# A two-layer graph network on one Trainium2 core: loop heads at the first slot of a fetch block, and basis values and window in PSUM

## The reference, cut to what matters

```python
basis = _basis(pseudo)                                   # edges x 9
messages = jnp.einsum('ek,ei,kio->eo', basis, x[row], weight)
out = jnp.zeros(...).at[col].add(messages)
out = out / jnp.maximum(degree, 1.0)[:, None]
out = out + x @ root_w.T + root_b

R = relu(abs_distances[:, None] @ w1 + b1) @ w2 + b2     # layer 2, per edge
acc = acc + _NORM[i] * jnp.einsum('euv,ef,evi,ofi->euo', Rb[..., k], Yf, Fb, C)
out = out.at[dst].add(msg)

x = _layernorm(x + layer1(x)); x = _layernorm(x + layer2(x))
```

## Time and profile before

| | us |
|---|---|
| median of 3 runs | 11979.86 (11974.05 to 11981.97) |
| the profiled execution | 12073.65 |
| span of its trace | 12071.8 |
| loop 1 (L363 first to L379 last) | 122.07 to 4941.83 |
| loop 2 | 5229 to 11990, about |

### The profile page before, as it was taken

How to read it: one execution, slowest core, us unless ns; L and a number is a source line. 1 busy time by engine, 2 the same in 40 slices (tenths; PEclk the granted TensorE clock), 3 DMA queues, 4 the chain that set the end, 5 groups by cost and what they waited for, 6 DMA issues and landing times. The chain is left out here.

```text
span 12071.8 us, 141219 instructions
## 1 busy us (share of the span) xinstructions
PE 8509.0 (70%) x44451; PEld 5928.2 (49%) x44451; DVE 5978.8 (50%) x14666; ACT 947.4 (8%) x3157; POOL 6732.9 (56%) x6757
## 2 busy tenths in 40 slices
PE   5777777777777777646666666666666667666676
PEld 5777777777676777523333333333333333333333
DVE  4333332333232323375666656566666666666665
ACT  0000000000000000001011011011101111110110
POOL 5777777677776777234444444444444444444442
PEclk5555555555555555578888888888888888888887
DMA  1000000000000000111111111111111111111111
GB/s 35 11 11 11 11 11 11 10 11 11 10 11 10 11 11 10 36 31 38 38 37 39 37 39 37 38 38 37 39 37 39 37 38 38 37 39 37 39 38 29
DMA packets 251984, 327.67 MB, mean 27 GB/s; under 512 B 110894, under 2 KB 160959, under 8 KB 251087
## 3 DMA queue, kind: packets, MB, share of 16 engines
q0 software_dynamic: 200000, 205.20, 9.1%
q1 hardware_dynamic: 51962, 122.18, 3.0%
HBM read 320.54 MB, written 6.40 MB: 27 GB/s over the span
## 5 line engine op out<-in xcount | busy, mean ns | idle before, releaser
L420 PE MATMUL sums_ps<-hot,spread 128*96 128x64 f32 (+1 forms) x18750 | 3232.9, 369 | 1021.1 <-DVE spread L370 768.9
L420 PEld LDWEIGHTS sums_ps<-hot,spread 128*96 128x96 f32 (+1 forms) x18750 | 3090.8, 280 | 1190.8 <-issue 699.0
L291 POOL DMA_INDIRECT rows<-in_x,idx_a x1875 | 2134.8, 1139 | 655.9 <-issue 588.7
L771 PE MATMUL radial_x<-edge_t,hidden 128*128 128x384 f32 x3750 | 1613.4, 571 | 1181.4 <-DVE edge_t L894 588.4
L291 POOL DMA_INDIRECT rows<-table_dram,idx_a x1875 | 1885.1, 1005 | 631.9 <-issue 533.3
L370 DVE TENSOR_TENSOR spread<-basis,rows 128x1440 f32<-128x1440 f32 x625 | 1037.5, 1660 | 2120.1 <-DMA rows<-in_x,idx_a 1420.6
L285 POOL COPY idx_a<-src_t 128x15 int32 x250 | 66.8, 267 | 3008.0 <-DVE edge_t L894 2524.3
L771 PE MATMUL radial_y<-edge_t,hidden 128*128 128x384 f32 x2500 | 1172.4, 599 | 772.7 <-DVE edge_t L894 419.0
L291 POOL DMA_INDIRECT rows<-in_x,idx_b x1250 | 1406.3, 1125 | 467.0 <-issue 413.2
L771 PEld LDWEIGHTS radial_x<-edge_t,hidden 128*128 128x128 f32 x3750 | 755.4, 216 | 1766.0 <-issue 791.1
L783 PE MATMUL sums_ps<-edge_t,hot 128*64 128x272 f32 x11000 | 1554.5, 430 | 12.2 <-DVE edge_t L910 12.1
(11 more groups left out here) (132 smaller groups left out, 5369.8 us busy)
## 6 DMA issues: line engine op xcount, KB each, us to landing
dist<-in_edge_weight SPq DMA_DIRECT2D x625, 160.0 KB, 3.1
rows<-in_x,idx_a POOLq DMA_INDIRECT x1875
rows<-table_dram,idx_a POOLq DMA_INDIRECT x1875
rows<-in_x,idx_b POOLq DMA_INDIRECT x1250
rows<-table_dram,idx_b POOLq DMA_INDIRECT x1250
acc<-in_edge_attr SPq DMA_DIRECT2D x1, 4687.5 KB
table_dram<-edge_t SPq DMA_DIRECT2D x1, 4687.5 KB
acc<-in_edge_attr SPq DMA_DIRECT2D x1, 3125.0 KB
```

The source lines that it names most:

```text
L291: pool.indirect_dma_start(out=rows[u if own else SLOT[u]][:, j, 0:width], out_offset=None, in_=table, in_offset=bass.IndirectOffsetOnAxis( ...
L420: last = pe.matmul(sums_ps[s][0:m, c * WINDOW:(c + 1) * WINDOW], spread[s][:, j, c * CH:c * CH + m], hot[s][:, j, :], start=(j == 0 and c ...
L771: last = pe.matmul(radial[h][:, j, 0:R], hidden[s][:, (j0 + j) * P:(j0 + j + 1) * P], w2p[:, :], start=True, stop=True)
```

## The change

The loops over the iterations get it on POOL, DVE, PE and ACT in loop 1 and on SP, ACT, POOL, PE and DVE in loop 2; PE's two have the hint. In `spline_edges` the three `basis` buffers leave SBUF and become three stretches of 45 columns in a PSUM bank of their own, `own_ps`, of which the first 64 columns take a copy of `window`. The copy is made once a pass, and DVE waits for it. Loop 2 goes on with `window` in SBUF.

```diff
+def near_loop(nc, eng, start, end, hint=False):
+    return nc.Fori(start, end, engines=bass.OrderedEngineSet([eng.engine]), head_slot={eng.engine: 0}, hint_back_edge=hint)
...
     with pool.Fori(0, passes) as p:
-        with pool.Fori(0, B) as i:
+        with near_loop(nc, pool, 0, B) as i:
...
-        basis = ring("basis", [P, G, 9])
...
+        own_ps = ctx.enter_context(nc.psum_tensor("own_ps", [P, 512], F32))
+        window_ps = own_ps[:, 0:WINDOW]
+        basis = [own_ps[:, WINDOW + n * 9 * G:WINDOW + (n + 1) * 9 * G].rearrange("e (t k) -> e t k", k=9) for n in range(SLOTS)]
...
-                dve.tensor_tensor(hot[s][:, :, :], keep["window"][:, :].unsqueeze(1).to_broadcast([P, G, WINDOW]),
+                dve.tensor_tensor(hot[s][:, :, :], window_ps.unsqueeze(1).to_broadcast([P, G, WINDOW]),
                                   rel_t[:, tiles].unsqueeze(2).to_broadcast([P, G, WINDOW]), ALU.is_equal).then_inc(hot_ready, 1)
...
                 dve.tensor_tensor(spread[s][:, :, 0:K].rearrange("e t (k c) -> e t k c", c=C),
-                                  basis[s][:, :, :].unsqueeze(3).to_broadcast([P, G, 9, C]),
+                                  basis[s].unsqueeze(3).to_broadcast([P, G, 9, C]),
                                   rows[s][:, :, :].unsqueeze(2).to_broadcast([P, G, 9, C]), ALU.mult).then_inc(spread_ready, 1)
...
                 next_pass(dve, keep, step, p * 2 + steps)
+                dve.tensor_copy(window_ps, keep["window"][:, :]).then_inc(window_ready, 1)
+                dve.wait_ge(window_ready, p + 1)
...
-                with dve.Fori(0, B - 1) as i:
+                with near_loop(nc, dve, 0, B - 1) as i:
                     body(i, False)
...
-                with pe.Fori(0, B - 1) as i:
+                with near_loop(nc, pe, 0, B - 1, hint=True) as i:
                     body(i, False)
```

More of the change, by code:

```diff
@@ L325, in spline_edges @@
         msg_ps = [ctx.enter_context(nc.psum_tensor(f"msg_ps{n}", [P, 512], F32)) for n in range(SLOTS)]
-        gathers_begun = sem("l0_gathers_begun")
+        own_ps = ctx.enter_context(nc.psum_tensor("own_ps", [P, 512], F32))
+        window_ps = own_ps[:, 0:WINDOW]
+        basis = [own_ps[:, WINDOW + n * 9 * G:WINDOW + (n + 1) * 9 * G].rearrange("e (t k) -> e t k", k=9) for n in range(SLOTS)]
+        gathers_begun, window_ready = sem("l0_gathers_begun"), sem("l0_window_ready")
         step, wk_landed, wk_ready, idx_ready = sem("l0_step"), sem("wk_landed"), sem("wk_ready"), sem("l0_idx_ready")
@@ L362, in build @@
                 dve.wait_ge(summed, freed(g, u))
-                dve.tensor_tensor(basis[s][:, :, :].rearrange("e t (a b) -> e t a b", b=3),
+                dve.tensor_tensor(basis[s].rearrange("e t (a b) -> e t a b", b=3),
                                   f[:, :, 0:3].unsqueeze(3).to_broadcast([P, G, 3, 3]),
                                   f[:, :, 3:6].unsqueeze(2).to_broadcast([P, G, 3, 3]), ALU.mult).then_inc(basis_ready, 1)
-                dve.tensor_tensor(hot[s][:, :, :], keep["window"][:, :].unsqueeze(1).to_broadcast([P, G, WINDOW]),
+                dve.tensor_tensor(hot[s][:, :, :], window_ps.unsqueeze(1).to_broadcast([P, G, WINDOW]),
                                   rel_t[:, tiles].unsqueeze(2).to_broadcast([P, G, WINDOW]), ALU.is_equal).then_inc(hot_ready, 1)
@@ L455, in _ @@
             with act.Fori(0, passes) as p:
-                with act.Fori(0, B) as i:
+                with near_loop(nc, act, 0, B) as i:
                     g = p * B + i
@@ L721, in _ @@
             with sp.Fori(0, passes) as p:
-                with sp.Fori(0, B) as i:
+                with near_loop(nc, sp, 0, B) as i:
                     g = p * B + i
@@ L812, in _ @@
                 body(0, True, False)
-                with pe.Fori(1, B - 1) as i:
+                with near_loop(nc, pe, 1, B - 1, hint=True) as i:
                     body(i, False, False)
@@ L962, in _ @@
                 body(0, True, False)
-                with dve.Fori(1, B - 1) as i:
+                with near_loop(nc, dve, 1, B - 1) as i:
                     body(i, False, False)
```

## The result

The changed kernel takes 12613.06 us (12598.09 to 12619.73, 4 runs) against 11976.95 us: ratio 1.0525, interval 1.0512 to 1.0538. It is 636 us slower; forecast was 195 us faster.

The account below looks back on a forecast made before the run. POOL's gathers, prolonged by DVE's spread, were taken to pace loop 1. From 12073.65, -194 (unblocked gathers, capped by PE's late posts) and +0.3 (copy) give 11880; less 93.8 to the median, 11785 us, range 11250 to 12180.

Parts of the forecast that it names:

- Part (1): Loop 1: with basis in PSUM the spread no longer blocks POOL's gathers; 600 us taken off POOL's time.
- The price of a PSUM operand: DVE's spread with basis in PSUM takes 1.66 to 1.78 us, hidden by POOL's pace; +75 us without that cover.
- Loop heads and hints: Both loops: no instruction is fetched there, so placed heads and hints give 0, with -20 to +20 us.
- the rival in its own form: Loop heads matter: late posts are PE waiting for instructions, and all would go; 9780 us or so, chance 0.06.
- (5): Loop 1: PE's late posts limit gathers to one each 1.48 us, 7.4 us a unit; 600 us shrink to 194.
- Slower, by unpaced gathers: Loop 1: with POOL less blocked, late posts stop everything; 8.0 to 8.2 us a unit, 12161 to 12286 us, chance 0.28.
- The signs named for this case: POOL's waits for spread well above 92 us, ACT waiting for remote in over 180 units, loop 1 over 4850 us.
- The distance to the median: Before's median lies 93.8 us below its profiled execution; the same was taken off 11880, giving 11786.
- the full gain of the lock: Loop 1: posts stay on time or cost no more than now; -600 us, 11380 us in all, chance 0.20.

Follow-up runs that it names:

- after_basis_sbuf: The changed kernel with the three basis buffers back in SBUF, window still in PSUM; on-time condition: 9559.90 us against 9553.77 for before, ratio 1.0008.
- heads_only: The kernel before with only the loop heads placed and the hints on PE's loops; late condition: 11982.60 us against 11982.08, ratio 0.9999.
- after_paced1: The changed kernel with a 128x128 fill on POOL behind each gather of loop 1; late condition: 12285.54 us against 11982.08 for before, ratio 1.0258.
- psum_only: The kernel before with basis and window in PSUM, loops placed as before; late condition: 12616.87 us against 11982.08, ratio 1.0527.
- after_fills12_b: The changed kernel with POOL fills of 256 columns (loop 1) and 280 (loop 2) behind each gather; late condition: 10207.58 us against 12027.50 for before.

## Why the prediction was wrong

**The lock, right.** Part (1) was to take 600 us off POOL; 587 us of busy time went in the late condition and 602 us of loop 1 where nothing else stood in the way. after_basis_sbuf shows that it is the spread's second SBUF input.

**The price of a PSUM operand, right.** The spread costs 1.65 us, just under the 1.66 to 1.78 taken: the operand in PSUM has no price here. Hot's 0.49 is unchanged, the copy takes 0.23 us once.

**Loop heads and hints, right.** Ratios 0.9999 and 1.0010. Refuted is the rival in its own form, that the late semaphores go when the heads are placed: with them placed they are late still. That PE stands for want of instructions in some other way is not: its gaps by "issue" are just such a standing. Against it speaks only that the DMA view of after has no instruction packet in loop 1 (200 to 5400 us).

**The sum's next term, wrong.** The step that failed is (5), "I take 1.48 us, 7.4 us a unit". The mechanism was named: late semaphores where gathers are dense. The limit came out about right too: at 1.41 us they are late, at 1.44 to 1.46 hardly any are, where I had put 1.48. That was in part luck, since it was taken from a mean in which blocked and free gathers mix; the free ones came each 1.25 us even then. What was wrong is the use of it. I treated the limit as a cap, as if POOL would settle at 1.48 us a gather and PE follow, 194 us gained. Nothing holds POOL at the limit: it issues at 1.25 us until its buffers are full, PE's semaphores are then up to 15 us late and PE itself stands between its matmuls, and when POOL stands, PE comes back and the cycle starts again. The unit takes 8.59 us and not 7.40, and loop 1 is 551 us longer. The time is that of burst plus stall, 32.7 + 10.6 us an iteration by POOL, or 30.4 us of work and 12.5 us of gaps by PE. The wait that the sum lacked is PE's own: the prediction names the waits of ACT, DVE and POOL, and has PE's work at 5.99 us a unit with nothing between the matmuls. Loop 2 had shown the pattern in the trace of before (a burst at 1.24 us, then waits of 5.9 and 11.7 us), and I used it as evidence for lateness but not for its price. As a price it would have given the sign but too much: 25 x 1.24 + 2 x 0.72 = 32.4 us and 17.6 us of waits are 50 us an iteration, measured are 43.

**The rival that came.** "Slower, by unpaced gathers" had the right mechanism, the chance 0.28 and the price 8.0 to 8.2 us a unit, from windows in which blocked and late gathers mix. Measured is 8.59. Those windows hold only the beginning of it, since the blocked gathers still broke up the bursts. The range ended at 12180, 433 us short. The signs named for this case came: POOL's waits for spreads 1320 us, ACT's remote waits 228, loop 1 over 4850 us.

**The distance to the median, counted twice in part.** Taking 93.8 us off is right where the sum starts from a long execution. But most of that length lay in loop 1: 4820 us, against 4743 in heads_only, whose times are those of before. Term (5) had already set this loop to 7.4 us a unit, whatever it had taken before, so some 77 us went off twice. That is an estimate from one trace each, and small beside the miss of 828 us. (Two slips on which nothing hangs: 7.6 us a unit is 11911 us and not 11930, and the wait that ends at 8004.08 ends 3.5 us after the last gather.)

**What no view of the trace of before told** is that its long waits are a condition and not the kernel. In the on-time condition the full gain of the lock, a rival with a chance of 0.20, comes out: it said -600 us, and the measured effect is -588 us.

Open: what makes PE's semaphores late, and PE stand, in one condition and not in the other, and whether one of the two causes the other. In the cycle shown ACT's copy is 2.9 us late already at 2010.73 (matmuls from 2002.70 to 2007.80), before PE's first gap of that cycle. The share of all this in loop 2 is 19 us of 54 in each iteration, far more than anything in the change. Shown is that within that condition the pace of POOL's gathers decides what it costs, by after_paced1 beside psum_only in one group, 4 executions each, and by after_fills12_b with one execution; that bytes don't matter much is only suggested (a gather of loop 2 moves three times as much as one of loop 1, 150 against 50 MB in like numbers of packets, and both loops show it).

## What to carry to other kernels

When a stall goes, ask not only who is late next but whether anything holds the freed engine back: an unpaced producer that outruns a limit doesn't run at the limit, it bursts and stalls, and can end below where it was. Price such a case from the stretch of the trace that already bursts, not from a mean; here that would have given an upper bound (50 us for the measured 43). And read the idle time of the engine that computes, too, when it is put down to "issue": here it fills loop 1 up to PE's whole time, and part of it stands in the first row of the page of after.

Keep one operand of a long VectorE operation in PSUM where GpSimd gathers beside it: that was worth 6.2% here in the on-time condition. And compare a change under more than one condition of the chip before believing its sign: this one is +5.3% in one and -6.2% in the other, and the fills of 256 and 280 columns the reverse.

## What the runs showed of the hardware

- The late semaphores: PE's matmuls end by their records, and the waiting engine starts up to 15 us later, while gathers are issued by POOL each 1.25 us. At 1.44 to 1.46 us next to nothing of it was left (in loop 2 38 remote waits of DVE's hot, at most 2.8 us). The same kernel on the same chip had it in one group of runs and not in another: 11982 and 9554 us. I had taken the waits in the trace of before for a property of the kernel.
- PE's gaps: in the late condition PE stands up to 3.3 us ahead of a matmul with no cause that the profile shows, 1561 us of loop 1 in after; in the on-time condition loop 1 has none in any trace. They tell the condition even where no remote wait is left (536 us in after_fills12_b).
- The Trainium skill, SBUF — State Buffer, "Who interferes with whom", gives the exclusive lock of the port pair as the single rule of contention. The runs agree on the lock (beside a spread with two SBUF inputs a gather takes 1.93 us in the mean and up to 2.43, with one 0.94). In the on-time condition nothing else is seen; in the late one something is, since loop 1 went 551 us the other way.
- Fills of 16 columns behind a gather cost 0.01 us of pace and those of 128 columns 0.08, although they are busy for 0.13 and 0.22 us: part of POOL's 0.30 us between gathers is free for other work.
- VectorE writes the basis to PSUM in 0.21 us, to SBUF in 0.20. That the trace of before couldn't tell.
